# Router matmuls split around the attended rows' transposes, and a reordered mixture of experts, in a two-layer cross-attention kernel

## What is computed

```python
x = x + cross_attention_0(layernorm(x), ctx, ctx)        # 16 heads of 16, 64 context rows per batch
x = x + expert_choice_ffn(layernorm(x), Wr, br, ...)     # each of 8 experts takes its 1024 best rows
x = x + cross_attention_1(layernorm(x), ctx, ctx, masks)
x = x + zone_ffn(layernorm(x), Wg, Wu, Wd, Wr, ...)      # all 8 experts, weighted row by row
```

## Time and profile before

| | |
|---|---|
| median of 3 runs | 2432.75 us (2430.27 to 2434.61) |
| profiled execution | 2435.47 us, span 2433.4 us |
| mean granted TensorE clock | 0.961 |
| busy: PE, PEld, DVE, ACT, POOL | 91%, 79%, 60%, 35%, 15% of the span |
| attention 0: one turn of the loop | 23.55 us |
| attention 1: one turn of the loop | 25.9 us |

### The profile page before, as it was taken

How to read it: one execution, slowest core, us unless ns; L and a number is a source line. 1 busy time by engine, 2 the same in 40 slices (tenths; PEclk the granted TensorE clock), 3 DMA queues, 4 the chain that set the end, 5 groups by cost and what they waited for, 6 DMA issues and landing times. The chain is left out here.

```text
span 2433.4 us, 40395 instructions
## 1 busy us (share of the span) xinstructions
PE 2219.9 (91%) x15335; PEld 1921.7 (79%) x15335; DVE 1457.9 (60%) x3137; ACT 862.1 (35%) x1210; POOL 374.4 (15%) x352
## 2 busy tenths in 40 slices
PE   6999998646999949999997799999999999999998
PEld 5888887425888837787786688888888888888887
DVE  6787876585544447777775774554554455455454
ACT  2455554124444404444443432222222222222222
POOL 3111110105665431111110400000000000000000
PEclk9999999767999979999998899999999999999999
DMA  2121211204443321111111400000000000000000
GB/s 74 53 78 55 74 61 53 57 0 121 96 89 57 58 52 45 61 52 69 60 44 53 138 27 27 27 27 9 19 27 26 27 27 27 26 27 27 27 10 9
DMA packets 110137, 115.05 MB, mean 47 GB/s; under 512 B 16080, under 2 KB 98768, under 8 KB 110032
## 3 DMA queue, kind: packets, MB, share of 16 engines
q1 hardware_dynamic: 97744, 96.49, 12.6%
q0 software_dynamic: 12288, 17.05, 4.2%
HBM read 62.92 MB, written 50.59 MB: 47 GB/s over the span
## 5 line engine op out<-in xcount | busy, mean ns | idle before, releaser
L1878 DVE TENSOR_TENSOR zmix_hid<-zmix_act_gate,psum 128x1024 f32<-128x1024 f32 x128 | 156.3, 1221 | 373.2 <-issue 346.7
L143 PE MATMUL psum<-zmix_wd_hi,zmix_hid_hi 128*128 128x256 f32 x1024 | 289.7, 283 | 2.2 <-DVE zmix_acc L1869 1.9
L145 PE MATMUL psum<-zmix_wd_hi,zmix_hid_lo 128*128 128x256 f32 x1024 | 289.9, 283 | 0.0
L144 PE MATMUL psum<-zmix_wd_lo,zmix_hid_hi 128*128 128x256 f32 x1024 | 289.9, 283 | 0.0
L1829 ACT ACTIVATE zmix_hid_hi<-zmix_hid 128x1024 fp32r<-128x1024 f32 x128 | 135.5, 1059 | 393.5 <-PE psum L145 282.3
L1821 ACT ACTIVATE zmix_act_gate<-psum 128x1024 f32<-128x1024 f32 x128 | 131.7, 1029 | 379.4 <-PE psum L145 379.4
L604 PE MATMUL psum<-att_v_cur,att_probs 128*128 128x96 f32 x2048 | 252.7, 278 | 4.5 <-ACT att_probs L732 3.1
L604 PEld LDWEIGHTS psum<-att_v_cur,att_probs 128*128 128x128 f32 x2048 | 240.8, 193 | 14.6 <-ACT att_probs L732 4.0
L1883 DVE TENSOR_TENSOR zmix_hid_lo<-zmix_hid,zmix_hid_hi 128x1024 fp32r<-128x1024 f32 x128 | 158.9, 1242 | 135.1 <-ACT zmix_hid_hi L1829 134.1
L1869 DVE SCALAR_TENSOR_TENSOR zmix_acc<-psum,zmix_weight,zmix_acc 128x256 f32<-128x256 f32 x512 | 211.7, 476 | 1.6 <-PE psum L145 1.6
L143 PE MATMUL psum<-zmix_xT_hi,zmix_wg_hi 128*128 128x512 f32 x512 | 201.8, 394 | 10.7 <-DVE zmix_xT_lo L1858 10.7
(11 more groups left out here) (295 smaller groups left out, 4486.2 us busy)
## 6 DMA issues: line engine op xcount, KB each, us to landing
x<-att_x_new SPq DMA_DIRECT2D x32, 512.0 KB, 2.9
att_x_in<-in_x SPq DMA_DIRECT2D x16, 512.0 KB, 3.9
rows<-att_normed_new SPq DMA_DIRECT2D x16, 512.0 KB, 3.0
att_x_in<-x SPq DMA_DIRECT2D x16, 512.0 KB, 3.8
turned<-att_newT SPq DMA_DIRECT2D x16, 512.0 KB, 2.8
zmix_xn<-turned SPq DMA_DIRECT2D x16, 512.0 KB, 4.5
zmix_acc<-x SPq DMA_DIRECT2D x16, 512.0 KB, 4.2
out_x<-zmix_acc SPq DMA_DIRECT2D x16, 512.0 KB, 3.2
```

The lines of the kernel that those rows point to most:

```text
L143: pe.matmul(out, st_hi, mv_hi, start=first, stop=False)
L144: pe.matmul(out, st_hi, mv_lo, start=False, stop=False)
L145: return pe.matmul(out, st_lo, mv_hi, start=False, stop=last)
L1878: dve.tensor_tensor(hid[:, :, :], act_gate[:, :, :], psum[:, 2:4, :], ALU.mult).then_inc(up_out, 1)
```

## The change

Attention. `route` takes the tiles that it is to do. In `body`, tiles 0 and 1 of the batch in front are done ahead of `turn_attention`, tiles 2 and 3 where all four were. The logits go to bank 6, so `route` first waits for the normalise step of the current batch's tile 2 (the last reader of bank 6), and `outputs` waits for the logits' copy ahead of tile 0.

Mixture of experts. POOL issues the first two halves' gathers ahead of its six memsets, and TensorE's wait for the memsets moves from the start of the stage into `down`. The second expert's down weights are split, on ScalarE and VectorE, after the group's first hidden block, where before they were split at the end of the group in front. At the start VectorE splits the first rows ahead of the first down weights.

```diff
@@ attention, tensor engine
             def outputs(b):
                 pe.wait_ge(a_lo, done(KC, b, KC))
                 for t in range(TT):
-                    if t == 2:
+                    if t == 0:
                         after(pe, lg_out, b)
...
-            def route(b, p):
-                pe.wait_ge(new_out, b + 1)
-                for t in range(TT):
+            def route(b, p, tiles):
+                if 0 in tiles:
+                    pe.wait_ge(new_out, b + 1)
+                    if there(b + 1):
+                        pe.wait_ge(av_taken, done(TT, b + 1, TT - 1))
+                for t in tiles:
                     for c in range(KC):
-                        m = pe.matmul(psum[:, 7, t * PE_COLS:(t + 1) * PE_COLS], newT[:, p, c, t * P:(t + 1) * P], kv["wr"][:, c, :],
+                        m = pe.matmul(psum[:, 6, t * PE_COLS:(t + 1) * PE_COLS], newT[:, p, c, t * P:(t + 1) * P], kv["wr"][:, c, :],
                                       start=(c == 0), stop=(c == KC - 1))
-                m.then_inc(lg_made, 1)
+                if TT - 1 in tiles:
+                    m.then_inc(lg_made, 1)
...
+                if there(b - 1):
+                    route(b - 1, 1 - p, range(0, 2))
                 turn_attention(b)
                 if nxt:
                     turn_maxima(b + 1)
                 if there(b - 1):
-                    route(b - 1, 1 - p)
+                    route(b - 1, 1 - p, range(2, 4))
@@ mixture of experts, GpSimd
+            for h in range(2):
+                gather(0, 0, h)
             for p in range(2):
                 pool.memset(mid_lo[BIAS_ROW:, p, FC - 1, :].bitcast(F32), 0.0).then_inc(cleared, 1)
...
             pool.wait_ge(cleared, 6)
-            for h in range(2):
-                gather(0, 0, h)
@@ tensor engine
             def down(g, j):
                 p, i = j % 2, j // 2
+                if j == 0:
+                    pe.wait_ge(cleared, 6)
...
-            pe.wait_ge(cleared, 6)
             turn(0, 0, 0)
@@ scalar engine
                 for j in range(GJ):
                     hidden(q * GJ + j, j % 2, q * EP + j // 2)
+                    if j == 0:
+                        act.wait_ge(down_made[1], q * (EP * HT))
+                        down_weights(q * EP + 1, 1)
                 if not last:
                     up_weights(q + 1)
-                    for i in range(EP):
-
-                        act.wait_ge(down_made[1], q * (EP * HT) + (i + 1) * HT)
-                        down_weights(q * EP + EP + i, i)
+                    act.wait_ge(down_made[1], q * (EP * HT) + HT)
+                    down_weights(q * EP + EP, 0)
...
             down_weights(0, 0)
-            down_weights(1, 1)
@@ vector engine
+                    if j == 0:
+                        down_weights(q * EP + 1, 1)
                     if j >= 1:
                         out(j - 1)
...
                 out(GJ - 1)
-                if not last:
-                    down_weights(q * EP + EP + 1, 1)

             up_weights(0)
+            rows_lo(0, 0, 0, 0)
             down_weights(0, 0)
-            rows_lo(0, 0, 0, 0)
-            down_weights(1, 1)
```

## The result

| | before | after |
|---|---|---|
| median | 2433.68 us (2430.27 to 2435.78, 4 runs) | 2402.76 us (2400.26 to 2407.3, 4 runs) |
| profiled execution, span | 2435.47, 2433.4 us | 2402.14, 2400.1 us |
| attention 0, first scores to the end of the turns (15 turns) | 353.7 us | 342.5 us |
| attention 1, the same | 387.1 us | 376.0 us |
| start of the mixture of experts (POOL's first instruction to the first up product) | 16.84 us | 13.65 us |

A forecast was written before the change was run, and what follows sets the result against it. TensorE was taken as the bound, so time falls only in its waits or in work movable into them. Attention 22.7, mixture start 3.2 and between groups 3.3 sum to 29.2 us: median 2403.5, range 2396.5 to 2415.

The forecast's parts named there:

- Attention: Attention tail: half the router matmuls fill TensorE's idle place, so scores start 0.81 us earlier, 28 times: 22.7 us, floor 18.2.
- The squeeze at the transposes of the input rows: Attention turn: these transposes, after the scores, wait for aT_lo; ScalarE's exponentials cover this, so the whole 0.81 us is kept.
- rival 3: Attention tail: the first eight router matmuls don't fit, attended rows' transposes 0.96 us late, 0.15 lost a turn: 2430.4 us; chance 0.03.
- Start of the mixture: First gathers ahead of POOL's six memsets bring the start of the mixture of experts forward: 3.2 us, from 1 to 4.2.
- Between the groups: Three places between weight groups: moving the second expert's split shortens POOL's chain to the gathered rows: 3.3 us, -1.5 to +7.
- The chain on POOL: Between groups, eight scatter-adds then four gathers lead to the rows; with VectorE's split moved out, 3.1 us less together.
- The copy of indices: Third place between groups: a copy on POOL held beside VectorE's split, 0.99 us against 0.19 in the open: 0.8 gained.
- The gathers: Between groups: gathers after the adds may also escape VectorE's smaller subtractions, 0.6 us each place, counted only as upside.
- one slow stretch: Between groups: lower TensorE clock after the xT_lo wait, about 1.6 us, hidden by the rows' wait, might come into the open.
- 1, the port plays no part: Between groups: the adds' length has another cause, only attention and the start gain: 2406.8 us, up to 2410.5; chance 0.22.
- 2, another bound of the turn: Attention loops: VectorE's chain or aT_lo holds the turn: 2408 us at the floor, 2415 with half given back; chance 0.12.
- 4, half clock in the tail: Attention tail: splitting the router work drops TensorE's clock, 2.9 us a turn, 82 in all: 2508 us; chance 0.04.

The follow-up runs named there:

- e1: The attention part of the change alone, mixture of experts as in the kernel before: 2413.82 us, ratio 0.9919 to the kernel before.
- e10: The changed kernel with one router tile ahead of the attended rows' transposes and three behind: 2413.43 us, ratio 0.9912 to the kernel before.
- e11: The changed kernel with three router tiles ahead of the attended rows' transposes and one behind: 2404.82 us, ratio 0.988 to the kernel before.
- e3: The kernel before with only the first gathers ahead of POOL's memsets and the wait for these in the down products: 2430.92 us, ratio 0.9992.
- e5: The kernel before with only VectorE's split of the second expert moved, and its new order at the start: 2438.96 us, ratio 1.0009.
- e6: The changed kernel with two extra VectorE subtractions of two SBUF operands at a group's end: 2411.03 us, ratio 0.9899 to the kernel before.
- e7: The changed kernel with two extra VectorE reductions of one SBUF operand at a group's end: 2406.63 us, ratio 0.9881 to the kernel before.

## Why the prediction was right, and where it was off

**Attention: right, in size too.** Forecast 28 x 0.81 = 22.7 us. The 14 turns of each loop gave 11.07 + 10.88 = 21.95, 0.79 and 0.78 a turn, and e1 gave 21.8 with nothing else changed. The points named for the changed profile are met: no idle time before L616, scores 0.05 after the copy, turns of 22.76 and 25.13 us (forecast 22.7 and 25.1). The squeeze at the transposes of the input rows was covered, as the first turn had shown. e10 supports the size: router matmuls that end after the maxima's copy stand on the path. With half as many moved ahead a turn is 0.34 us longer (9.4 / 28), where 0.4 had been expected.

One step of the reasoning was too tight. I counted a late L616 as a loss one for one (rival 3's loss of 0.15 us a turn, and e11's forecast of 13 to 14 us). e11 moves it by 0.43 and loses nothing in the turns: the last maxima release L566.

**Start of the mixture: right, and on average a little too large.** Forecast 3.2 (1 to 4.2); the start took 13.65 us in place of 16.84 (3.2) in after. But over the ten profiles with POOL's new order it took 13.63 to 15.27 us (mean 14.5), over the four with its old order 16.84 to 16.93: 2.4 us on average. Alone this is below what the times resolve. The memsets end at 561.1 by POOL's rows of after, ahead of the first down product at 580.8: they cost nothing.

**Between the groups: the mechanism right, the term mis-sized.** Forecast 3.3 us (bounds -1.5 and +7); measured 9.6 between the two profiles, above the upper bound. The new code took 284.0 to 286.7 us in eight profiles (mean 284.7), the old one 294.1, 291.9 (e1) and 290.4 (e3): a mean gain of 7.5, and 3.7 at the least. Two parts of the term were too small.

*The chain on POOL*, from the start of the last add to the end of the fourth gather behind it, was put 3.1 us shorter over the three places. It took 10.15, 10.40 and 9.43 us and takes 7.84, 7.88 and 7.82: 6.4 less. In the first place it ended at 656.09 + 0.95 before, and ends at 642.70 + 0.94 now. Timeline of before, the first place's fourth gather and the second place's last add:

```profile
656.09 0.95 POOL L1319 DMA_INDIRECT moe_rows<-rows,moe_idx_get  x1 [0.30 <-issue]
...
720.23 2.97 POOL L1333 DMA_INDIRECT x<-moe_y,moe_idx_add  x1 [0.30 <-issue]
```

The adds gave 1.15 and 1.42 us, near the forecast. The copy of indices, forecast with 0.8, gave nothing. I had set its 0.99 us against 0.19, but here its row begins while the add ahead of it still runs: in e5, with no such subtraction beside it, it takes 0.77 or 0.78 in this place. After, it is held in all three places (1.05, 1.08 and 1.12 us), since the hidden block's subtraction now comes earlier. The gathers, which I had put at nothing with 0.6 a place upwards, gave 4.6: four of them took 5.32, 5.32 and 5.65 us and take 3.88, 3.89 and 3.91.

*The clock.* I had priced one slow stretch at 1.6 us, hidden ahead of the rows, and feared that it would come into the open. There were three, one in each place, and the two others already followed the wait for the rows. Windows of before:

```profile
732.50:738.00 5.50, 5.41 (x21) 4.55 (x22) 3.75 (x4) 0.69 (x1) 3.84 (x5) 0.69 0.36 98
806.90:814.00 7.10, 7.00 (x28) 5.79 (x29) 3.65 (x4) 2.17 (x3) 2.94 (x4) 0.76 0.29 78
```

By length times what is missing from 1.00, each costs 1.7 us: 4.70 x 0.36, 5.50 x 0.31 and 7.10 x 0.24. With one wait of 1.7 to 1.9 us in a place, the clock didn't fall at all. So the second group took 73.37 us and takes 71.13, 2.2 less by the chain's 2.3; the third 75.39 and 71.13, 4.3 less by 2.5 + 1.7; the fourth 73.70 and 70.66, 3.0 less by 1.6 + 1.7. Counted on TensorE it is the same sum: the waits fell from 9.25 to 5.34 us, 3.9 less, and 5.1 of the other 5.7 us are the clock. How often the clock falls differs between runs of the old code, three times in before, twice in e1 and once in e3, so part of the 9.6 is the one execution.

**The rivals.** *1, the port plays no part*: refuted by e5 (2.71 to 1.56 with the split gone) and by the pair e6 and e7. In all 14 profiles 52 adds start inside a VectorE subtraction of two SBUF operands, and every one of them takes 1.98 to 2.97 us; the other 844 take 1.55 to 1.65. The Trainium skill, "SBUF — State Buffer", section "Who interferes with whom", infers that a subtraction of two SBUF operands doesn't hold up the writing of descriptors; here the adds and gathers that start beside one do take longer (1.98 for 1.56, 1.93 for 0.95), so the measurement decides. The same section of the Trainium skill says that a VectorE instruction with two SBUF inputs contends with a GpSimd instruction that reads SBUF, and that a reduction never contends; both fit e6 and e7. Whether it is the reading of the indices that is held was not tried. *2, another bound of the turn*: not met, 21.95 of 22.7 us came. *3*: refuted by the row of L616. *4, half clock in the tail*: the granted clock (after the five busy times) is 1.00 in both loops of after, as before:

```profile
70.00:390.00 320.00, 313.89 (x2911) 277.12 (x2910) 260.98 (x751) 170.99 (x304) 55.47 (x56) 1.00 0.21 66
...
920.00:1280.00 360.00, 356.36 (x3186) 295.63 (x3179) 270.32 (x795) 175.68 (x311) 53.84 (x53) 1.00 0.17 60
```

That the median came out within 0.8 us of the forecast 2403.5 is partly luck. The gain of 30.9 us is 1.7 above the forecast of 29.2, and its parts miss by more: 0.7 us too much for attention, about 0.8 too much for the start, 4 to 6 too little between the groups, while executions differ by 3 to 4 us in the preparation alone.

## What to carry to other kernels

Before moving work into an idle place, follow the wait behind it on every engine: the shortest way to a shorter turn was not to fill TensorE's gap but to bring forward the one VectorE step that the next turn hangs on. Keep VectorE's two-operand SBUF work away from a chain of indirect DMAs on GpSimd, or give it one operand. Where several short waits stand close together, count the clock they cost as well as their own time: here each fall cost 1.7 us, about as much as a wait. That merging waits is what keeps the clock up is not shown; in e1 a single wait of 2.50 us had 0.63 behind it.

## What the runs showed of the hardware

- An indirect DMA of GpSimd that starts inside a VectorE subtraction of two SBUF operands ends late. In the 14 profiles all 52 such adds end 1.43 us after the end of the subtraction, whenever they started (1.98 to 2.97 us, for 1.55 to 1.65). The 293 gathers that start inside one, at least 0.05 us behind its start and 0.2 ahead of its end, end 0.8 to 0.9 us after it, for a usual 0.95. In e6, where one row holds two subtractions, the held add ends 1.43 after the first.
- One that had already started is not held: 1.56 us for the add of e6 that started 0.67 ahead. Nor is one beside a reduction (e7), a scaling or copy out of PSUM, or a subtraction with one operand in PSUM (0.94 to 1.04 us for gathers, 1.55 to 1.59 for adds).
- TensorE's granted clock stayed 1.00 behind single waits of 1.71 to 1.90 us, was 0.64 behind 1.84 us, and 0.78 and 0.76 behind waits of 3.21 and 3.17 us. The length of the last wait alone doesn't order these: in e3 one wait of 2.51 us had 0.73 behind it and one of 2.50 us had 1.00. What else does was not tested.
- The preparation ahead of the first scores takes 46.2 us or 3 to 4 more, whatever the kernel. Its cause is open.
